# Gated cross-attention and FFN layers on one core: second products by tokens, norms in pairs, a new planner and half the fillers

## The reference, cut to what matters

```
x = x + tanh(g_xattn[l]) * attention_l(layernorm(x), ctx)
x = x + tanh(g_ffn[l])   * ffn_l(layernorm(x))
ffn_0 = relu(h @ w1 + b1) @ w2 + b2
ffn_1 = sum_top2 w_e * (silu(h @ gate_e) * (h @ up_e)) @ down_e + sigmoid(h @ sg) * shared(h)
ffn_2 = relu(relu(h @ w1_e + bias1_e) @ w2_e + bias2_e), e = argmax router(h)
attention_3: slots = gru(softmax(q(rmsnorm(slots)) k^T over the slots, normalised) v, slots), 3 times
ffn_3 = round(h / s) @ round(rhs / r)^T * s * r
```

## Time and profile before

| what | value |
|---|---|
| three timed runs | 361.87, 360.57, 361.77 us; median 361.77 |
| the profiled execution | 361.95 us, its span 360.2 us |
| instructions | 5043 |
| mean granted TensorE clock | 0.987 |
| loads | 8.68 MB moved, nearly all of it in the first 27 us |

### The profile page before, as it was taken

One profiled execution on the slowest core, in us unless ns is written; L12 is line 12 of the kernel. 1 busy time (PEld: TensorE's weight loads), 2 busy tenths in 40 slices (PEclk: granted clock), 3 DMA queues, 4 the chain that ended last, 5 costly groups with the idle time before them and its releaser, 6 DMA issues.

```text
span 360.2 us, 5043 instructions
## 1 busy us (share of the span) xinstructions
PE 328.1 (91%) x1843; PEld 175.3 (49%) x1843; DVE 225.3 (63%) x635; ACT 136.9 (38%) x287; POOL 47.8 (13%) x73
## 2 busy tenths in 40 slices
PE   0789989998888899999999997899999999999994
PEld 0455453463424543554444434455445677677442
DVE  2596574366628551677766728345353797798995
ACT  1226326331451565225321361711232366646200
POOL 6113112031010100010200020101021311101110
PEclk9999999998989999999999999999999999999998
DMA  7940000000000000000000300000000000000001
GB/s 195 354 198 0 2 0 2 1 0 3 0 2 0 2 0 0 2 0 1 1 2 0 118 11 0 2 0 2 0 0 0 2 1 2 0 2 0 0 14 47
DMA packets 6669, 8.68 MB, mean 24 GB/s; under 512 B 2907, under 2 KB 5493, under 8 KB 6389
## 3 DMA queue, kind: packets, MB, share of 16 engines
q1 hardware_dynamic: 6645, 8.37, 7.0%
HBM read 7.84 MB, written 0.52 MB: 23 GB/s over the span
## 4 chain that ended last, share of the span: by engine, by line
PE 76%; DVE 15%; ACT 6%; issue 1%; DMA 1%; SPq 0%; DVEq 0%; ACTq 0%
PE psum L754 68%; DVE mx L1443 6%; ACT wide L1124 4%; PE psum L838 3%; DVE wide L1610 1%; PE psum L956 1%; PE psum L874 1%; DMA w_attn<-in_attn 1%; PE psum L1052 1%; PE psum L1079 1%; ACT xn_t L1124 1%; PE psum L791 0%; DVE rinv_d L1452 0%; DVE wide L1575 0%; DVE rinv L1449 0%
## 5 line engine op out<-in xcount | busy, mean ns | idle before, releaser
L754 PE MATMUL psum<-xn_t,w_ffn 128*128 128x512 f32 (+1 forms) x136 | 66.6, 608 | 0.8 <-ACT xn_t L1124 0.8
L754 PE MATMUL psum<-wide,w_ffn 128*128 128x512 f32 (+1 forms) x92 | 47.4, 603 | 0.5 <-DVE wide L1535 0.3
L754 PE MATMUL psum<-halves 128*128 128x512 bf16 x178 | 43.9, 379 | 0.2 <-DVE q_lo L1435 0.2
L1443 DVE TENSOR_REDUCE mx<-psum 128x4 f32<-128x308 f32 x96 | 38.7, 471 | 7.3 <-PE psum L754 7.1
L1124 ACT ACTIVATE wide<-psum 128x512 f32<-128x512 f32 x72 | 36.6, 624 | 11.0 <-PE psum L754 10.8
L1124 ACT ACTIVATE q<-psum 128x512 f32<-128x512 f32 (+1 forms) x40 | 23.5, 594 | 44.1 <-PE psum L754 43.8
L754 PEld LDWEIGHTS psum<-xn_t,w_ffn 128*128 128x128 f32 (+1 forms) x136 | 24.9, 190 | 28.8 <-issue 25.9
L698 POOL TENSOR_SCALAR nw<-mv 128x4 f32<-128x4 f32 x16 | 3.6, 227 | 218.7 <-DVE mv L1309 218.7
L754 PEld LDWEIGHTS psum<-halves 128*128 128x128 bf16 x178 | 17.3, 99 | 17.2 <-issue 1.7
L1315 DVE TENSOR_SCALAR xn<-x,mv,nw 128x128 f32<-128x128 f32 x64 | 17.8, 347 | 10.9 <-POOL nw L699 10.7
L754 PE MATMUL psum<-w_attn,q 128*128 128x128 f32 x192 | 23.7, 276 | 0.2 <-DVE q L1459 0.2
(11 more groups left out here) (208 smaller groups left out, 492.5 us busy)
## 6 DMA issues: line engine op xcount, KB each, us to landing
w_ffn<-in_ffn SPq DMA_DIRECT2D x1, 2088.5 KB, 12.6
w_ffn<-in_ffn SPq DMA_DIRECT2D x1, 1104.0 KB, 5.0
w_attn<-in_attn SPq DMA_DIRECT2D x1, 640.0 KB, 8.1
w_attn<-in_attn SPq DMA_DIRECT2D x2, 288.0 KB, 5.8
x<-in_x SPq DMA_DIRECT2D x2, 256.0 KB, 3.1
w_ffn<-in_ffn SPq DMA_DIRECT2D x1, 512.0 KB, 6.7
out<-x SPq DMA_DIRECT2D x2, 256.0 KB, 2.3
rows<-in_rows SPq DMA_DIRECT2D x1, 468.0 KB, 6.0
```

Of the source, the lines that this page charges most:

```text
L754: return nc.tensor.matmul(out_, lhs, rhs, start=start, stop=stop, **kw)
L1443: last = V.tensor_reduce(mx[:, b, t, lane_heads(g)], banks.bank("max", layer, b, t, g)[:, 0:GK].rearrange("p (h k) -> p h k", k=CTX), AX.X ...
```

## The change

- Second products (`down0`, `down_shared`, `down1`, `down2`) go by tokens: the 128x128 block of activations is stationary, the weights move, and the result is tokens by features, as x lies. A product with zeros opens the bank. The evictions to `y_t` and `back` on PE are gone; DVE adds from PSUM. Only stage 5 still has an eviction, for its Relu.
- `spread` uses transposes in place of products with the identity.
- `norm` on DVE and POOL and `norm_end` work on two tiles at a time. In stage 7 ACT scales, DVE quantises, ACT's eviction takes the rounding constant off, and DVE clips both ways in one step on the bf16 result.
- `gru_z`'s product is POOL's.
- The planner has a step for each engine's part with its own list of what it comes after, and takes from all of them the smallest `at + later - LEFT * left`, where left is the longest chain of estimated times behind the step. LAG and the preferences are gone. It counts 0.095 us where PE changes between whole-array, row-tiled and column-tiled products, and holds the times at which loads land. Gate and up products, sums and values, and the three hidden products of the GRU are steps of their own. `LATER` has new entries.
- Fillers are put for an idle time by the same formula with FILLER = 0.44, into the bank that is free first, and eight wide ones run at the start on a tile of zeros.
- Loads: x of half 0, columns, identity and query weights first; x of half 1 later; the second experts' weights go over the first attention's and first FFN's weights and the masks, after the first FFN of both halves.

```diff
-FILLER = 0.22
+FILLER = 0.44
+WARM_UP = 8
+LEFT = 0.2
+SWITCH = 0.095
...
+                at = max([steps[key].end for key in st.after], default=0.0) - LEAD.get(st.key[:2], 0.0)
+                at = max(at, free[st.engine], LOADED.get(st.key, 0.0))
+                if st.engine == "pe" and tiling(st.phase, st.args)[0] != tiled:
+                    at = max(at, free["pe"] + SWITCH)
...
+                    rank = at + st.later - LEFT * st.left
...
+                (bank, earlier), since = banks.first_free(drained)
+                idle = at - max(free["pe"], since) - FILLER
+                if idle >= FILLER:
+                    fillers[st.key] = bank, earlier, int(idle / FILLER)
...
             load_x(0)
+            sp.dma_start(cols[:, :], a["cols"]).then_inc(loaded["cols"], 16)
+            sp.dma_start(consts[:, 0:P], a["consts"][:, 0:P]).then_inc(loaded["ident"], 16)
+            sp.dma_start(packs["attn0"][:, 0:wq_n], a["attn0"][:, 0:wq_n]).then_inc(loaded["wq0"], 16)
             sp.dma_start(ctx_t[:, :], a["ctx_t"]).then_inc(loaded["ctx_t"], 16)
...
             for b in range(B):
-                sp.wait_ge(*banks.full("y", 3, b))
+                sp.wait_ge(*banks.full("out", 1, b))
             sp.dma_start(packs["ffn2"][:, :], a["ffn2"]).then_inc(loaded["ffn2"], 16)
...
+            def norm(b, stage, h):
+                tiles = slice(2 * h, 2 * h + 2)
+                pool.wait_ge(var_ready[b], 2 * stage + h + 1)
+                link(G.tensor_scalar(nw[:, b, 0, tiles], mv[:, b, tiles, 1], LN_EPS, None, ALU.add))
+                G.tensor_tensor(nw[:, b, 2, tiles], nw[:, b, 0, tiles], minus_half[:, tiles], ALU.pow)\
...
+            def gru_z(b, it):
+                pool.wait_ge(z_ready[b], it + 1)
+                G.tensor_tensor(kept[:, b, :, :], tz[:, b, :, :], slots[:, b, :, :], ALU.mult).then_inc(kept_ready[b], 1)
...
-                    last = mm(bk[:, t * P:(t + 1) * P], rinv_d[:, b, t, :], ident)
+                    last = nc.tensor.transpose(bk[:, t * P:(t + 1) * P], rinv_d[:, b, t, :], ident)
...
-                done = mm(bk, weights[0:n, i * D:(i + 1) * D], wide[0:n, b, at_, :], start=i == 0, stop=last)
+                if i == 0:
+                    mm(bk, zeros16[:, :], halves[:, 0:S], stop=False)
+                by_tokens(bk, wide[0:n, b, at_, :], weights[0:n, i * D:(i + 1) * D], last)
+
+            def by_tokens(bk, source, weights, last):
+
+                for t in range(T):
+                    done = mm(bk[:, t * P:(t + 1) * P], source[:, t * P:(t + 1) * P], weights, start=False,
+                              stop=last and t == T - 1)
...
+            def scaled(b):
+                act.wait_ge(centre_ready[b], 1)
+                for t in range(T):
+                    last = A.activation(xn[:, b, t, :], x[:, b, t, :], ACT.Identity, bias=nw[:, b, 0, t:t + 1],
+                                        scale=nw[:, b, 2, t:t + 1])
...
-            def gru_z(b, it):
-                dve.wait_ge(z_ready[b], it + 1)
-                V.tensor_tensor(kept[:, b, :, :], tz[:, b, :, :], slots[:, b, :, :], ALU.mult)
...
             def gru_end(b, it):
                 dve.wait_ge(n_ready[b], it + 1)
+                dve.wait_ge(kept_ready[b], it + 1)
+                dve.wait_ge(z_ready[b], it + 1)
```

More of the change, by code:

```diff
@@ L110 @@
+FFN2_LOADS = 12.0
+OF_CHUNKS = {"sums": "sum", "values": "pv"}
+DOWN = {"down0": C0, "down1": C1, "down2": C2 + 1, "down_shared": len(SHC)}
+SHARED = len(SHC)
+PIECES = SHARED + C1
+LATER = {
[34 rows of a table added]
 }
 class Step:
[L118 to L121, removed]
@@ L124, in stream_steps, with __init__ @@
[L124 to L145, removed]
+    def __init__(self, key, us, after):
+        self.key, self.us, self.after = key, us, after
+        self.engine, self.phase, self.half, self.args = key[0], key[1], key[2], key[3:]
+        self.later, self.left, self.end = 0.0, us, None
@@ new lines, in all_steps, with chain, step, of @@
+def all_steps():
+    steps = {}
+    def chain(b):
+        def step(phase, *args, after=(), then=None, **takes):
+            previous = list(after)
+            for engine, us in takes.items():
+                key = engine, phase, b, *args
+                steps[key] = Step(key, us, previous + (then or {}).get(engine, []))
+                previous = [key]
+        return step
+    prepare_steps(chain(PREPARATION))
+    for b in range(B):
+        half_steps(b, chain(b))
+    return steps
+def of(b):
+    return lambda engine, phase, *args: (engine, phase, b, *args)
@@ L162, in attention @@
+        step("max_rows", layer, after=[at("dve", "maxima", layer, T - 1)], pe=0.45, act=0.5)
         for j in range(NJ):
-            step("scores", layer, j, on=True, pe=0.95 if layer else 1.95, act=1.95, after=[(PREPARATION, "masks")])
+            ready = [at("act", "max_rows", layer), at("dve", "query", layer), prepared("pool", "keys_in", layer)]
+            if not layer:
+                ready.append(prepared("act", "masks"))
+            step("scores", layer, j, after=ready + in_order("pe", "scores", layer, j), pe=0.95 if layer else 1.95, act=1.95)
@@ L164, in attention @@
         for j in range(NJ):
[L165 to L170, removed]
+            evicted = {"act": 0.5} if j == NJ - 1 else {}
+            for phase, made in (("sums", 0), ("values", layer)):
+                step(phase, layer, j, after=[at("act", "scores", layer, j), prepared("dve", "values_in", made)]
+                     + in_order("pe", phase, layer, j), pe=0.86, **evicted)
@@ L175, in stream_steps @@
[L175 to L182, removed]
-    attention(2, 1)
[L184 to L187, removed]
@@ new lines, in half_steps @@
+    step("back", 1, after=[at("pe", "down0", C0 - 1), at("pool", "bias", 1)], dve=0.65)
+    norm(2, [at("dve", "back", 1)])
+    attention(2, 1)
+    turn(3)
+    step("gates1", after=[at("act", "turn", 3)], pe=0.92, dve=3.0, act=0.2)
+    step("weights_turn", after=[at("act", "gates1")], dve=1.97, pe=0.43, act=0.5)
+    for k in range(PIECES):
+        step("gate", k, after=[at("act", "turn", 3)] + in_order("pe", "gate", k),
+             then={"act": in_order("act", "gate", k) + ([at("dve", "up", k - 2)] if k > 1 else [])}, pe=0.86, act=0.5)
+        step("up", k, after=[at("act", "turn", 3)] + in_order("pe", "up", k),
+             then={"dve": in_order("dve", "up", k) + [at("act", "gate", k)]}, pe=0.86, dve=0.6)
@@ new lines, in half_steps @@
+    step("slots_back", after=[at("dve", "gru_end", ITERS - 1)], dve=0.65)
+    norm(7, [at("dve", "slots_back")])
+    turn(7)
+    step("quantised", after=[at("dve", "turn", 7), prepared("dve", "slots_in", 4)], pe=0.25, dve=1.83)
+def schedule():
+    steps = all_steps()
+    for b, tenths in LATER.items():
+        for st, later in zip([st for st in steps.values() if st.half == b], tenths):
+            st.later = later / 10
+    followers = {key: [] for key in steps}
+    for st in steps.values():
+        for key in st.after:
+            followers[key].append(st)
+    for st in reversed(list(steps.values())):
+        st.left = st.us + LANDS[st.engine] + max([other.left for other in followers[st.key]], default=0.0)
@@ L316, with tiling @@
+    return orders, banks.dealt, fillers
+def tiling(phase, args):
+    if phase in ("maxima", "scores"):
+        whole = "whole" if args[0] == 0 else "rows"
+        return (whole, "rows") if phase == "scores" else ("rows", whole)
+    return ("columns", "columns") if phase in OF_CHUNKS else ("whole", "whole")
 class BankTurn:
```

601 lines of the change are left out of this document (309 added, 292 removed), and 49 rows, old and new, of the table LATER.

## The result

The changed kernel took 350.39 us (median of four runs, 349.39 to 351.49) against 361.82 for the kernel before in the same session: a ratio of 0.969 (95% interval 0.965 to 0.974). The forecast was 338, the range 323 to 356. The profiled execution took 349.42 us, its span 347.6, 12.6 less than the span of before.

The account below looks back on a forecast made before the run. Bounds: start, latency and DVE; 20 to 280 us, PE with 22 us of idle time and fillers; behind 280, DVE and hops between engines. Sum: -3.5 - 5 + 0 - 9 - 4.9 - 1.5 = -23.9 from 361.95, so 338 us; range 323 to 356.

Parts of the forecast that it names:

- The iterations: Three recurrent iterations of both halves: one product per half and iteration moves from DVE to POOL, round 19.5 to 17.9, -4.9 us.
- the POOL lock: Iterations: POOL's product may hold the port pair shared with DVE for its whole length; taken as 0, 7.6 us kept for range.
- My upper bound, +7.6: Iterations: if each of six products moved to POOL held DVE for its length, 6 x 1.27 us; sum 346, not 338.
- Fewer fillers: Whole kernel: filler runs end where work is ready, so halving the fillers gains only where a run is too long: 0.
- the rival of the clock: With fewer fillers, PE's clock falls to 1.2 GHz in the iterations (+18) and body (+14): slower, 368 us, chance 0.08.
- The start: Up to first maximum: reordered loads and DVE steps bring it from 17.04 to about 11.5 us; -5, bounds 0 and -6.
- Products by tokens: Second products, nearly all between 20 and 280 us: transposes and spread records leave, zero products come; -3.5 us of PE.
- the bound of +7: Products by tokens: upper bound if the first weight load of each product isn't hidden, 0.15 x 48 us; none taken.
- Paired norms: Norms split into two of two tiles, POOL's instructions run twice: 0, +-2 us for the handful on the path.
- Order: Between 20 and 280 us: finer engine-by-engine order and shorter chains take 9 off 22 us idle and fillers; bounds -22, +30.
- The tail: End of kernel: DVE's 2.9 us wait in half 1 falls as scalings go to ACT; -1.5 us, bounds +1 and -3.
- the signs that I named: Trace signs: first maximum near 11.5 us, no transposes, 0.112 records, 18 us round, DVE over 85%, less PE idle, clock above 0.95.

Follow-up runs that it names:

- the version with the warm start: Changed kernel with product on DVE, FILLER 0.22, four fillers ahead of each iteration's first update product, plus two before first transposes and two before first query: 344.93 us, ratio 0.954.

## Why the prediction failed, step by step

*The iterations* (forecast -4.9, measured +2.2) are the step that failed. It said that 0.68 us leaves DVE in each half and iteration and shortens the round by as much, that DVE's share stays, and that the POOL lock is taken at 0 "since at that point DVE mostly reads PSUM". That DVE's work counts is right: with four products gone altogether, about their 2.7 us came. But moved is not gone. The very next DVE steps (L1720, L1721) read two SBUF operands, three of the six met POOL's product, and the six second steps took 7.0 us where they take 4.2; in the kernel before, the product had mostly lain in a wait for ACT, and moving it gained 0. The move cost 2 us in the changed kernel and nothing measurable beside enough fillers, where 4.9 of gain stood in the sum. My upper bound, +7.6, had the mechanism and its price; the value that I took from it had not. Of the 7.1 us between forecast and result, 3.7 are the fall of the clock (13.5 for a step of 9.84), which belongs to the next term, and 3.4 are this term's own. That is an estimate from single executions. Undone with enough fillers, the iterations take 48.0 us, 2.6 fewer than before the change.

*Fewer fillers* (forecast 0) failed too: 3 to 4 us lost, shown by the constant alone. The half that I wrote was 36 of 178, and none in the iterations: I had not worked out what the rule leaves. What it costs was in the rival of the clock, but as an event of 18 us or nothing. It came as falls of 12 to 16 us, of which the one at 288 to 300 counted; more fillers and no lock together took it away, in the profiled executions either alone only moved or shortened it. The sign had been there: the wait ahead of the fall at 84 us, which I took for some 2 us, is 0.78 in the earlier trace rows.

*The start* (-5, measured -4.1): mechanism right. The rest is the clock: warmed, the first maximum comes at 11.76, beside my 11.5.

*Products by tokens* (-3.5, with the zeros at 8 x 0.216). The price of a pitch holds:

```profile
72.65 3.73 PE L854 MATMUL psum<-early,wide 128*128 128x128 f32 x32
```

This is 3.73 less a last record of 0.28 over 31, 0.11 each, with the weights changed for every one, so the weight loads are hidden and the bound of +7 was empty. PE work in the body counts at 0.7 to 0.9 by the run with more zeros, which makes this term -2.4 to -3.2; the products themselves I did not undo.

*Paired norms* (0, bounds 2): -1.5 to -2.3 by the run with whole norms, at the edge of the bounds. *Order* (-9): what is left of the body's -10.1 is some -5; that is a remainder and no run shows it by itself. The two traces agree with it: from the first maximum to the first transposes PE was idle 15.6 us and had 33 fillers (7.1) before, and is idle 16.5 with 6 fillers (1.3) now, 4.9 less together. So the order was oversized, and part of what it was to bring came by the norms.

*The tail* (-1.5, measured -0.6): DVE's wait of 2.9 us is gone, as said:

```profile
325.60 0.63 ACT L1377 ACTIVATE wide<-wide 128x512 f32<-128x512 f32 x1 [4.01 <-DVE wide L1714]
...
326.34 0.69 DVE L1720 TENSOR_TENSOR wide<-wide 128x512 f32<-128x512 f32 x1
```

The step now starts 0.1 after ACT's tanh. But the end didn't come as much earlier, and the clock is not the reason: it is 0.83 in this tail of 31.05 us, and 0.96 in the version with the warm start, where the tail takes 31.65. What limits it I did not test.

Of the signs that I named, first maximum (12.97, warmed 11.76), pitch and missing transposes came. A shorter round, DVE over 85% (it was 40.94 of 52, 79%), PE idle well under 15 us in the body (15.5 of 244) and a clock above 0.95 behind 280 did not, and "DVE steps beside POOL's product stretched" was on the list of what would be wrong. The fastest version that leaves nothing out is the one with the constant 0.22, the product on DVE and fillers at the start and ahead of the updates: 344.93 us, 1.5% under the changed kernel and 4.6% under the one before.

## What to carry to other kernels

Work moved from one engine to another that shares something with it is not removed: look in the trace for one pair of the two side by side, and if the one waited for the other there, put that price in the sum, not only in the range. Look also whether the moved work had stood in a wait for a third engine: then there is nothing to gain. Where PE waits, its clock may fall behind the wait, as it did here after 1.88 us, so the price of fillers belongs to each wait of PE and not to their total. Before costing a constant that thins something out, work out what its rule leaves.

## What I had not expected of the hardware

- POOL and DVE took turns in both orders: POOL's product took 1.27 alone, 1.92 with a whole DVE step inside it and 1.52 where it began in the middle of one; DVE's step took 0.69 alone and 1.64 behind POOL.
- A body at a clock of 0.51 from 84 to 98 us cost nothing that could be measured, while a fall at 288 to 300 made one step 13.5 us long instead of 9.84.
- POOL's power takes 0.72 us for two columns and 1.04 for four.
- Four fillers of 128x512 in gaps of 0.8 and 0.7 us raised the clock at 8 to 12 us from 0.62 to 1.00.
